# TensorE's fillers in the opening become 16-bit products of ones, and q's turn moves behind the probabilities' turns in layer 1

## The reference

```
x = x + tanh(g_xattn[0]) * xattn0(layernorm(x), ctx)   # 32 heads, 8 kv heads, width 128, q and k rms-normed
x = x + tanh(g_ffn[0])   * lora_experts(layernorm(x))  # 8 experts of rank 16, softmax router
x = x + tanh(g_xattn[1]) * xattn1(layernorm(x), ctx)   # 16 heads, 4 kv heads, width 96
x = x + tanh(g_ffn[1])   * swiglu(layernorm(x))        # hidden 1792
# xattn: q = x Wq; k, v = [ctx; x] Wk, Wv; softmax(q k^T / sqrt(d)) v, times Wo
```

## Time and profile before

| | us |
|---|---|
| median of 3 runs | 1152.05 (1151.71 to 1152.43) |
| the profiled execution | 1151.04 |
| its span | 1149.2 |
| TensorE busy | 1117.6 (97%) |
| VectorE busy | 829.5 (72%) |
| ScalarE busy | 837.8 (73%) |
| GpSimd busy | 377.8 (33%) |

### The profile page before, as it was taken

How to read it: one execution, slowest core, us unless ns; L and a number is a source line. 1 busy time by engine, 2 the same in 40 slices (tenths; PEclk the granted TensorE clock), 3 DMA queues, 4 the chain that set the end, 5 groups by cost and what they waited for, 6 DMA issues and landing times.

```text
span 1149.2 us, 22754 instructions
## 1 busy us (share of the span) xinstructions
PE 1117.6 (97%) x7160; PEld 706.1 (61%) x7160; DVE 829.5 (72%) x1996; ACT 837.8 (73%) x2759; POOL 377.8 (33%) x674
## 2 busy tenths in 40 slices
PE   7789999999999999999999999899999999899998
PEld 5456665666566656665666666667667666455554
DVE  5878777777767767777687878887778788744444
ACT  6978888888888888888887777788787776522221
POOL 5663434336633343333335443212121212110000
PEclk8999999999999999999999999999999999999999
DMA  7676654554655645656364675778987695310000
GB/s 255 136 156 117 136 139 117 127 115 110 135 143 97 144 122 132 141 93 161 85 132 93 106 148 113 153 133 194 226 183 151 134 188 110 82 28 1 37 1 37
DMA packets 418328, 141.13 MB, mean 123 GB/s; under 512 B 392993, under 2 KB 402977, under 8 KB 418209
## 3 DMA queue, kind: packets, MB, share of 16 engines
q1 hardware_dynamic: 416304, 136.01, 54.6%
q0 software_dynamic: 1904, 3.67, 1.2%
HBM read 39.21 MB, written 2.10 MB: 36 GB/s over the span
## 4 chain that ended last, share of the span: by engine, by line
PE 78%; DVE 10%; issue 3%; POOL 3%; ACT 3%; DMA 2%; SPq 0%; DVEq 0%; POOLq 0%; ACTq 0%
PE bank L599 22%; PE bank L601 22%; PE bank L600 22%; PE bank L801 8%; PE bank L820 5%; DVE pieces L1179 2%; DVE mx L1280 1%; DVE stats L1190 1%; DVE x L1315 1%; ACT probs L998 1%; ACT junk L895 1%; POOL rstd L1583 1%; DMA k_weight<-in_k_norm_w 1%; DVE q_rows L1179 1%; DVE oT L1179 1%
## 5 line engine op out<-in xcount | busy, mean ns | idle before, releaser
L998 ACT ACTIVATE probs<-bank,nb,rq 128x256 f32<-128x256 f32 x256 | 141.4, 564 | 40.8 <-DVE nb L1285 39.8
L1179 DVE SCALAR_TENSOR_TENSOR pieces<-probs,rs,pieces 128x256 f16<-128x256 f32 x384 | 166.6, 493 | 4.9 <-ACT pieces L892 2.5
L892 ACT ACTIVATE pieces<-probs,rs 128x256 f16<-128x256 f32 x384 | 166.1, 522 | 2.8 <-DVE rs L1295 0.8
L1280 DVE TENSOR_REDUCE mx<-bank 128x2 f32<-128x512 f32 x192 | 131.1, 683 | 47.8 <-PE bank L601 47.4
L895 ACT ACTIVATE junk<-bank 128x128 bf16<-128x128 f32 x384 | 101.7, 288 | 45.4 <-PE bank L601 44.4
L599 PE MATMUL bank<-wq,xT 128*128 128x512 f16 (+1 forms) x352 | 126.7, 360 | 0.0
L601 PE MATMUL bank<-wq,xT 128*128 128x512 f16 (+1 forms) x352 | 126.6, 360 | 0.0
L600 PE MATMUL bank<-wq,xT 128*128 128x512 f16 (+1 forms) x352 | 126.6, 360 | 0.0
L599 PE MATMUL bank<-wo,oT 128*128 128x512 f16 x320 | 121.3, 379 | 2.8 <-DVE oT L1179 2.3
L1179 DVE SCALAR_TENSOR_TENSOR q_rows<-bank,q_rows 128x512 f16<-128x512 f32 (+1 forms) x96 | 62.1, 646 | 82.3 <-ACT junk L895 79.7
L601 PE MATMUL bank<-wo,oT 128*128 128x512 f16 x320 | 121.3, 379 | 0.0
(11 more groups left out here) (218 smaller groups left out, 2804.4 us busy)
## 6 DMA issues: line engine op xcount, KB each, us to landing
raw_o<-in_wo_a SPq DMA_DIRECT2D x8, 1024.0 KB, 6.3
raw_q<-in_wq_a SPq DMA_DIRECT2D x7, 1024.0 KB, 6.0
raw_kv<-in_wkv_a SPq DMA_DIRECT2D x8, 512.0 KB, 4.4
turned<-pieces SPq DMA_TRANSPOSE x192, 2.8
raw_q<-in_wq_c SPq DMA_DIRECT2D x4, 768.0 KB, 4.9
raw_o<-in_wo_c SPq DMA_DIRECT2D x4, 768.0 KB, 5.1
down_rest<-in_down_t POOLq DMA_DIRECT2D x5, 512.0 KB, 4.0
ff_in<-in_gate_t SPq DMA_DIRECT2D x4, 448.0 KB, 3.8
```

The lines of the kernel that those rows point to most:

```text
L892: return act.activation(out, in_, ACT.Copy, scale=scale)
L998: act.activation(probs[:, h, :], bank[h // 2][:, (h % 2) * KV:(h % 2 + 1) * KV], ACT.Exp, bias=nb[:, h:h + 1], scale=scale, accum_out=sums ...
L1179: return dve.scalar_tensor_tensor(out, in_, scale, hi, ALU.mult, ALU.subtract)
L1280: dve.tensor_reduce(mx[:, pr], chunks(bank[i][:, :], 2), AX.X, ALU.max, negate=True).then_inc(mx_done, 1)
```

## The change

`awake` now multiplies the bf16 ones by themselves, 128 columns, into a bank that is handed to it. Where 22 and 10 transposes stood, 52 and 28 products stand, and the first of these groups waits for two constants instead of five. Four new groups come ahead of waits: 22 in the middle of `kv_proj(3)`, 32 ahead of `scores(1)`, 24 ahead of `project(0)`, 32 in `values(1)`. For these, `values` now waits for the turned probabilities behind its other waits, and `project(0)` waits for k's norms first. The banks are ones that are free or of which other columns are in use.

In SyncE's step, from step 64 on, the order k, q, probabilities 0, probabilities 1 becomes k, probabilities 0, probabilities 1, q.

```diff
--- before.py
+++ after.py
@@ -522,13 +522,23 @@
                     turn_norm(0, norm0)
                 if norm1 is not None:
                     turn_norm(1, norm1)
-                if T < N:
-                    turn_k(T)
-                if T < N - 1:
-                    turn_q(T)
-                if S < N:
-                    turn(S, 0)
-                    turn(S, 1)
+                if n < N0:
+                    if T < N:
+                        turn_k(T)
+                    if T < N - 1:
+                        turn_q(T)
+                    if S < N:
+                        turn(S, 0)
+                        turn(S, 1)
+                else:
+                    if T < N:
+                        turn_k(T)
+                    if S < N:
+                        turn(S, 0)
+                    if S < N:
+                        turn(S, 1)
+                    if T < N - 1:
+                        turn_q(T)
                 if norm2 is not None:
                     turn_norm(2, norm2)
                 for kind, load in (("kv", load_kv), ("q", load_q), ("o", load_o)):
@@ -606,9 +616,10 @@
             def tile_of(src, k, t):
                 return tuple(w[:, k, t * P:(t + 1) * P] for w in src)
 
-            def awake(n):
+            def awake(n, out):
+
                 for _ in range(n):
-                    pe.transpose(bank[4][:, 0:P], ident[:, :], ident[:, :])
+                    pe.matmul(out[:, 0:P], ones[:, :], ones[:, :], start=True, stop=True)
 
             def norm_turn(k, t):
                 pe.wait_ge(norm[k].xn, t + 1)
@@ -631,6 +642,8 @@
                 if t == 0 and first:
                     pe.wait_ge(wkv_done, 2 * g + 2)
                 for i in sources:
+                    if n == 3 and i == 1:
+                        awake(22, kv_bank(n))
                     if n < NT and i == 0:
                         pe.wait_ge(ctx_lo, t + 1)
                     if n < NT and i == 1:
@@ -664,6 +677,8 @@
 
             def scores(n):
                 L = layer_of(n)
+                if n == 1:
+                    awake(32, kv_bank(3))
                 pe.wait_ge(kturned, 16 * (n + 1))
                 pe.wait_ge(qturned, 16 * (n + 1))
                 if n >= 1:
@@ -677,13 +692,15 @@
 
             def values(n):
                 L = layer_of(n)
-                for i in range(2):
-                    pe.wait_ge(pturned[i], 16 * (n + 1))
                 if n == 0:
                     pe.wait_ge(qlo_done, 2)
                     pe.wait_ge(qsq_done, 2 * NH)
                 if n >= 1:
                     pe.wait_ge(olo_done, n)
+                if n == 1:
+                    awake(32, bank[4])
+                for i in range(2):
+                    pe.wait_ge(pturned[i], 16 * (n + 1))
                 for kt in range(2):
                     last = mm3(bank[4][0:L.hd, :], [w[:, kt, 0:L.hd] for w in v[n % VS]],
                                [turned_out[:, n % 2, c, kt] for c in range(2)], start=kt == 0, stop=kt == 1)
@@ -691,11 +708,12 @@
 
             def project(n):
                 L, (g, t) = layer_of(n), place(n)
+                if n == 0:
+                    pe.wait_ge(kn_done, 8)
+                    awake(24, y_bank(n))
                 pe.wait_ge(olo_done, n + 1)
                 if L is L1:
                     pe.wait_ge(omoved[n % 2], 16 * L1.oc * ((n - N0) // 2 + 1))
-                if n == 0:
-                    pe.wait_ge(kn_done, 8)
                 if n == N - 5:
                     pe.wait_ge(vlo_done, 2 * N)
                 elif n == N - 4:
@@ -822,15 +840,16 @@
                         if m == MT - 1 and i == 1:
                             last.then_inc(ff_down, 1)
 
+            pe.wait_ge(consts, 2)
+            awake(52, bank[4])
             pe.wait_ge(consts, 5)
-            awake(22)
             norm_turn(0, 0)
             pe.wait_ge(ssq_kv, 2)
             pe.matmul(bank[0][:, SUMS:SUMS + 2], ones[:, :], ssq[:, 0:2], start=True, stop=True).then_inc(sum_kv, 1)
             norm_turn(0, 1)
             pe.wait_ge(ssq_c, 1)
             sum_squares(bank[1][:, 0:1], C_SUM, 1).then_inc(sum_c, 1)
-            awake(10)
+            awake(28, bank[4])
             kv_proj(0, (1,), last=False)
             pe.wait_ge(ssq_q, 2)
             pe.wait_ge(nrm_kv, 1)
```

## The result

The changed kernel took 1154.44 us (median of 20 runs), the kernel before beside it 1152.01 us (20 runs): ratio 1.0026, 95% interval 1.0019 to 1.0033. It is slower, by 3.0 us by this ratio (the two medians lie 2.4 apart), where 1149.0 was forecast. The profiled execution took 1154.16 us, its span 1152.4.

A forecast was written before the change was run, and what follows sets the result against it. TensorE, busy 1117.6 of 1149.2 us, was taken as the bound, leaving idle time and low-clock losses to gain. −2.5 (opening), −0.8 (turns) and +0.2 (tail) sum to −3.1: forecast 1149.0 us, range 1147.3 to 1152.3.

The forecast's parts named there:

- The clock in the opening: First projection, from 13.34 us: 28 products before it keep the clock at 2.4 GHz; −2.5 us, bounds 0 and −2.9.
- a start that comes earlier by x comes out at 697 us as x: TensorE from 77 to 697 us: no idle time named, so an opening gain carries through in full.
- The products at the start and the fillers at no cost: Opening groups of 52 and 28 and four later fillers: all end within existing waits; cost 0.
- The wait at 860.93: Layer 1: TensorE's 0.81 us wait for the probabilities' turns goes, as they are issued 1.33 earlier; −0.8 us.
- The rival of fillers that outlast their waits: Four later fillers at low clock or without overlapping weight loads end after their waits: 1155.2 us; chance 0.10.
- the one on q's turn: Layer 1: q's turn, issued later, makes ScalarE wait about 1 us, with room behind; order −0.8, bounds to +1.
- The tail: Layer 1's end: move of o 1.0 later, pushed into 2.25 us idle ahead of 979.04; +0.2, bounds 0 and +1.0.
- the turns' order costs what it brings: Layer 1: the 860.93 wait stays in another step and 1.0 at 971.43 reaches the end: 1150.5 us; chance 0.15.
- The mean of 1 to 2 us: Opening clock gain: by the skill's rule of a moving clock change, 2.5 is a run's upper figure, this its mean.

The follow-up runs named there:

- e6: The unaltered changed kernel measured again on another chip, against the kernel before: 1155.99 us, ratio 1.0041.
- e9: Fillers alone, with SyncE's layer 1 order as before, repeated on another chip against the kernel before: 1150.46 us, ratio 0.9988.
- e14: The whole change with 66 products instead of 28 in the opening's second group, against the kernel before: 1149.22 us, ratio 0.9988.
- e15: The kernel before with SyncE's new order, 62 products in the opening and none of the four later groups: 1159.06 us, ratio 1.0060.

## Why the prediction was wrong, step by step

- *The clock in the opening* ("Two of three, so I expect it held"): half right. It was held over the idle time of 2.38 and fell at 14.9. The third tile's norm came 0.6 earlier, not 2.5, so that the lead at 74.57 was 2.3 all the same is luck: the rest came from waits that the forecast left out, 1.24 ahead of 47.22 and 1.50 ahead of 76.87 before. The loss was read from one profile, too. Of the four profiles with the old opening two have a low clock before 20 us and two have none; of the ten with the change's opening, four and six. Fillers alone measured a gain of 1.4 us (1150.24 to 1148.86) and 1.9 (1152.31 to 1150.46).
- *"a start that comes earlier by x comes out at 697 us as x"*: wrong. The 2.3 at 74.57 came out as 1.0 at 696.66, lost in part to waits for turned probabilities that only the earlier start has.
- *The products at the start and the fillers at no cost*: right. 28 took 1.72 us from the first to the end of the last; idle time was left ahead of all four waits (0.21, 1.02, 0.27, 0.57), against 0.3, 0.9, 0.5 and 0.5 forecast. The rival of fillers that outlast their waits is out.
- *The wait at 860.93*: right, it is gone (−0.8); 0.79 at 822.57 and 0.30 at 857.04 came in its stead, so little is gained.
- *The step that failed* is the one on q's turn: "it waits about 1 us, and with it the next high parts of the probabilities. These have room". The wait of about 1 us was right for a landing of 2.7 to 3.3. But the wait was treated as an offset that is taken once, and the order was put at −0.8 with +1 as the upper bound, while it closes a ring whose length is 5.0 us and the landing; beside the fillers alone it cost 5.5 us (e6 and e9). The room was 8.48 − 7.8 = 0.7 us at a landing of 2.8, and the landings of before already ran to 5.7: the row that would have warned stood there and only its lower half was used. The very turn that was reckoned with, that of 854.28 before, took 5.0 us to land in the trace of the kernel before, with a packet of q8 in it. Before, 4.5 to 8 us passed from q's turn until its rows were written again; after, 2.9 to 5.4.
- *The tail* (+0.2): not as forecast. Two waits, 1.53 and 0.71, stand ahead of the 1.33 for the moved o, and the idle time of 2.25 that was to absorb it shrank to 1.28 without absorbing the delay, since the turn that ends it was late itself.
- *The rivals*: "the turns' order costs what it brings" came nearest, with the order at +1.0 us where 4.9 were lost. None had the fillers and the order acting on each other.
- *Edits priced one by one and added.* Measured, the parts are 0.9986 and 0.9998, and together 1.0026. What the fillers change in layer 1 is TensorE's lead and when its instructions are brought in; e14 and e15 point to the second.

The trace also lets the Trainium skill be weighed where the prediction used it ("TensorE: Matmul & The Clock Gate", section "What's actually happening"): that the moment of the clock's change moves between runs is what the executions here show, but by more than half a microsecond. With the same opening the clock was low from 14.9 to 18.2 in the change's profile and not at all in e6's. The mean of 1 to 2 us that the prediction drew from it does not follow from the page.

## What to carry to other kernels

Before a transfer is moved behind others, follow what its landing lets go until the way comes back to its own issue, and compare the sum with the step for the longest landing that the profile shows, not for the median. Where there is one buffer behind such a transfer, double it before the order is touched. An edit that only adds instructions far away can move the packets that bring an engine's instructions: when parts that are harmless alone lose together, look for what shares the DMA engines in that stretch, and test with a changed count of fillers.

The best versions here are fillers alone (0.9986 and 0.9988) and the change with a second place for q's rows (0.9988) or with q's turn ahead from step 85 (0.9990); they don't differ measurably, so the new order brings nothing. The change with 66 fillers does as well in its short executions, and only because a packet happens to fall elsewhere.

## What was unexpected of the hardware

- A turn (DMA transpose) of q's rows lands in 2.7 to 2.8 us by itself. With a 16 KB packet of instructions between its issue and its landing the turn of the table took 4.3 to 6.5 (eight profiles), others 2.7 to 4.7 where no load of weights lay beside them. With a 512 KB load issued 0.2 us ahead to 0.5 behind it the turn took 4.7 to 5.4; issued 1.2 to 1.5 behind, with no packet, the load leaves it at 2.7 to 2.8. The packet was moved only by count and place, so why one stops the transfers for 1 us is open.
- The kernel before has such landings too (3.9 for the turn of 920.39, with a packet near 921); they are hidden, as q's turn goes out early.
